# Second self attention of a perceiver block: 64x64 score blocks, and another order of one loop on one Trainium2 core

## The reference

```python
qkv = einsum('bsh,oh->bso', x, w_qkv)      # 32 query heads, 4 key and 4 value heads, each 64 wide
q, k = rope(q, pos), rope(k, pos)          # rotary embedding; k, v are shared by 8 query heads
scores = einsum('bqhd,bkhd->bhqk', q, k) * 64 ** -0.5
scores = where(tril(64, 64), scores, lowest)
out = einsum('bhqk,bkhd->bqhd', softmax(scores), v)
return einsum('bso,ho->bsh', out.reshape(b, s, 2048), w_o)
```

## Time and profile before

| | us |
|---|---|
| median of 3 runs (2544.1 to 2547.37) | 2544.89 |
| the profiled execution's own time | 2557.27 |
| its span | 2555.5 |
| TensorE's matmuls busy in the span | 2288.6 (90%) |
| VectorE busy | 1629.1 (64%) |
| ScalarE busy | 1206.9 (47%) |
| GpSimd busy | 1034.5 (40%) |
| mean granted TensorE clock | 0.941 |

### The profile page before, as it was taken

The page is one execution under the profiler, slowest core; times in us unless marked ns, Lnnn a source line. Parts: engine busy times, 40 slices in busy tenths (PEclk is TensorE's granted clock), DMA queues, the critical chain, the costliest instruction groups (busy, mean ns, idle before and its releaser), DMA issues. The chain is left out here.

```text
span 2555.5 us, 45882 instructions
## 1 busy us (share of the span) xinstructions
PE 2288.6 (90%) x16212; PEld 1813.5 (71%) x16212; DVE 1629.1 (64%) x2618; ACT 1206.9 (47%) x2236; POOL 1034.5 (40%) x718
## 2 busy tenths in 40 slices
PE   4799999999996999969979999999999988888766
PEld 2677777777763888857757788888888866666644
DVE  5367887777785333334422788888788864666663
ACT  2355665666542333313213676666666652233242
POOL 4168988898882000001100455455444530011320
PEclk8799999999996999979999999999999988899889
DMA  3000000001001122114230000000000011111200
GB/s 111 26 2 27 27 27 12 17 27 48 2 1 35 62 66 66 37 22 95 66 108 17 27 27 18 12 27 27 19 10 27 1 66 39 38 37 33 80 1 17
DMA packets 104280, 89.92 MB, mean 35 GB/s; under 512 B 32752, under 2 KB 82432, under 8 KB 104080
## 3 DMA queue, kind: packets, MB, share of 16 engines
q1 hardware_dynamic: 103792, 87.28, 11.3%
q0 software_dynamic: 288, 0.00, 0.0%
HBM read 86.22 MB, written 1.05 MB: 34 GB/s over the span
## 5 line engine op out<-in xcount | busy, mean ns | idle before, releaser
L2276 POOL TENSOR_TENSOR xT<-xT,x1b_ring 128x512 f32<-128x512 f32 (+1 forms) x176 | 248.4, 1411 | 212.6 <-ACT x1b_ring L2406 205.7
L941 POOL TENSOR_TENSOR x0b_krstd<-x0b_krstd,minus_half 128x24 f32<-128x24 f32 x64 | 267.5, 4180 | 88.3 <-DVE x0b_krstd L1004 84.7
L961 POOL TENSOR_TENSOR xT<-xT,x0b_ring 128x512 f32<-128x512 f32 (+1 forms) x170 | 240.3, 1413 | 40.1 <-ACT x0b_ring L1178 25.4
L111 DVE TENSOR_TENSOR x1b_plo<-x1b_ring,x1b_phi 128x512 fp32r<-128x512 f32 (+1 forms) x208 | 222.0, 1067 | 5.3 <-issue 4.7
L2421 ACT ACTIVATE x1b_ring<-x_ps,x1b_keymask 128x512 f32<-128x512 f32 (+1 forms) x208 | 143.1, 688 | 130.5 <-DVE xT L2348 125.8
L1178 ACT ACTIVATE x0b_ring<-x0b_ring 128x512 f32<-128x512 f32 (+1 forms) x208 | 131.2, 631 | 150.1 <-DVE x0b_ring L1022 141.7
L1054 DVE TENSOR_TENSOR x0b_ring<-x_ps,x0b_krstd 128x512 f32<-128x512 f32 (+1 forms) x208 | 142.8, 686 | 75.4 <-PE x_ps L846 74.3
L116 PE MATMUL x_ps<-x1b_qy,x1b_yT 128*128 128x512 f32 (+1 forms) x416 | 175.1, 421 | 4.3 <-ACT x1b_ring L2421 2.9
L2348 DVE SCALAR_TENSOR_TENSOR xT<-x_ps,x1b_keymask,xT 128x512 f32<-128x512 f32 (+1 forms) x176 | 131.2, 746 | 57.6 <-PE x_ps L118 56.7
L116 PE MATMUL x_ps<-x1b_phi,x1b_yv 128*128 128x512 f32 (+1 forms) x416 | 165.8, 399 | 1.5 <-ACT x1b_out_sb L2388 1.5
L118 PE MATMUL x_ps<-x1b_qy,x1b_yT 128*128 128x512 f32 (+1 forms) x416 | 163.9, 394 | 0.0
(11 more groups left out here) (588 smaller groups left out, 5760.5 us busy)
## 6 DMA issues: line engine op xcount, KB each, us to landing
x_y<-in_ctx_dram SPq DMA_DIRECT2D x8, 1536.0 KB
x_y<-in_ctx_dram SPq DMA_DIRECT2D x24, 512.0 KB, 3.9
a_wn<-in_L_attn_W_Q_dram SPq DMA_DIRECT2D x16, 256.0 KB, 3.1
a_wn<-in_L_attn_W_K_dram SPq DMA_DIRECT2D x16, 256.0 KB, 3.4
a_wn<-in_L_attn_W_V_dram SPq DMA_DIRECT2D x16, 256.0 KB, 4.0
a_won<-in_L_attn_W_O_dram SPq DMA_DIRECT2D x16, 256.0 KB, 2.8
x1a_wq<-in_L_xattn_Wq_dram SPq DMA_DIRECT2D x4, 1024.0 KB, 10.6
x1c_wo<-in_L_xattn_Wo_dram SPq DMA_DIRECT2D x8, 512.0 KB, 6.9
```

What stands on the lines that cost most here:

```text
L111: return v.tensor_tensor(lo, exact, hi.bitcast(F32), ALU.subtract)
L941: ins = g_.tensor_tensor(r, r, c.minus_half[:, 0:8].unsqueeze(1).broadcast_to([P, whole, 8]), ALU.pow)
L961: g_.tensor_tensor(total[half][0:m, :], old, src, ALU.add).then_inc(summed, 1)
L2276: g_.tensor_tensor(total[half][0:m, :], old, src, ALU.add).then_inc(summed, 1)
```

## The change

The scores, their softmax and the probabilities keep only the 64x64 blocks within a sequence. S makes for each tile, head and sequence one 64x64 block, the second sequence of a tile on partitions 64 to 127 of the result, so that logits and probabilities are 128 x (4 x 64). The mask is loaded in two pieces of 64x64. F transposes two tiles' probabilities at once, so that keys of even tiles come to lie on partitions 0 to 63 and those of odd tiles on 64 to 127. C makes the values in the same places, in 64 token pieces. V multiplies first the even tiles and then, after a wait for its own first half, the odd ones, since both write the same partitions of the bank. In the order, Q goes ahead of V (and of C), and W ahead of R.

```diff
--- before.py
+++ after.py
@@ -2534,10 +2534,10 @@
         qT = [st.sb(f"qT{i}", [P, B * S]) for i in range(2)]
         kT = st.sb("kT", [P, B * S])
         vn = st.sb("vn", [P, T * HDR])
-        pT = [st.sb(f"pT{u}", [P, T * P]) for u in range(2)]
-        causal = st.sb("causal", [P, P])
+        pT = [st.sb(f"pT{u}", [P, T * S]) for u in range(2)]
+        causal = st.sb("causal", [P, S])
         ln = NormTranspose(st, c, ps)
-        sm = SmallSoftmax(st, HDR ** -0.5, causal[:, :].unsqueeze(1).broadcast_to([P, T, P]))
+        sm = SmallSoftmax(st, HDR ** -0.5, causal[:, :].unsqueeze(1).broadcast_to([P, T, S]), keys=S)
         wn_loaded = [st.sem(f"wn_loaded{u}") for u in range(2)]
         won_loaded = [st.sem(f"won_loaded{u}") for u in range(2)]
         kv_loaded, tables_loaded, zeroed = st.sem("kv_loaded"), st.sem("tables_loaded"), st.sem("zeroed")
@@ -2552,6 +2552,7 @@
         rotated = st.sem("rotated")
         apart = st.sem("apart")
         projected = st.sem("projected")
+        begun = st.sem("begun")
         full = [st.sem(f"full{i}") for i in range(4)]
         free = [st.sem(f"free{i}") for i in range(4)]
 
@@ -2564,9 +2565,10 @@
                     for w in text.split()]
 
 
-        HEAD = "N R1 R0 W O F0 F1 G S V C Q"
-        INNER = "N R0 W O F0 F1 G S V Q"
-        TAIL = "N R0 W A0 O F0 F1 G A1 S"
+
+        HEAD = "N W R1 R0 O F0 F1 G S Q V C"
+        INNER = "N W R0 O F0 F1 G S Q V"
+        TAIL = "N W R0 A0 O F0 F1 G A1 S"
         PAIRS = KVR * PAIRSR
         STEPS = KVR - 1
 
@@ -2574,10 +2576,10 @@
 
 
             if part == "prologue":
-                return (window(1, "A0 A1 W") + window(2, "B") + window(1, "Q") + window(2, "R1 R0 W G S C Q")
-                        + window(3, "N R0 W G F0 F1 S V Q"))
+                return (window(1, "A0 A1 W") + window(2, "B") + window(1, "Q") + window(2, "W R1 R0 G S C Q")
+                        + window(3, "N W R0 F0 F1 G S Q V"))
             if part == "body":
-                return (window(0, INNER) + window(1, TAIL) + window(2, "B") + window(1, "V Q") + window(2, HEAD)
+                return (window(0, INNER) + window(1, TAIL) + window(2, "B") + window(1, "Q V") + window(2, HEAD)
                         + window(3, INNER))
             return (window(0, INNER) + window(1, "N R0 O F0 F1 G S V") + window(2, "N O F0 F1 V")
                     + window(3, "O"))
@@ -2652,9 +2654,12 @@
 
                 load_kv(0)
                 load_query(0, 0)
-                for dst, src in ((turn, c.tables["turn"]), (cosine, c.tables["cosine"]), (sine, c.tables["sine"]),
-                                 (causal, c.tables["causal"])):
+                for dst, src in ((turn, c.tables["turn"]), (cosine, c.tables["cosine"]), (sine, c.tables["sine"])):
                     sp.dma_start(dst[:, :], src).then_inc(tables_loaded, 16)
+
+                for b in range(2):
+                    sp.dma_start(causal[S * b:S * b + S, :], c.tables["causal"][S * b:S * b + S, S * b:S * b + S]
+                                 ).then_inc(tables_loaded, 16)
                 load_query(1, 1)
                 load_out(0, 0)
                 load_out(1, 1)
@@ -2671,7 +2676,7 @@
             @block.gpsimd
             def _(g_):
                 ln.gpsimd(g_)
-                g_.wait_ge(tables_loaded, 64)
+                g_.wait_ge(tables_loaded, 80)
 
                 def body(part, i, first):
                     for off, op, k in plan(part):
@@ -2695,7 +2700,7 @@
                 pe.wait_ge(ln.xT_done, T)
                 pe.wait_ge(x_done, T)
                 pe.wait_ge(zeroed, 1)
-                pe.wait_ge(tables_loaded, 64)
+                pe.wait_ge(tables_loaded, 80)
                 for t in range(T):
                     pe.matmul(ps[:, 4 + t, :], zeros[:, :], xT[0][:, 0, :], start=True, stop=False,
                               skip_group_check=True)
@@ -2742,10 +2747,14 @@
                         if op == "C":
                             pe.wait_ge(kv_done, 2 * g + 2)
                             pe.sem_inc(apart, 1)
-                            for t in range(T):
+
+                            for n in range(T):
                                 for j in range(DC):
-                                    mm = pe.matmul(out[:, t * HDR:(t + 1) * HDR], c.xT[:, j, t * P:(t + 1) * P],
-                                                   wvT[:, j, :], start=(j == 0), stop=(j == DC - 1))
+                                    for r in range(2):
+                                        token = (4 * (n // 2) + 2 * r + n % 2) * S
+                                        mm = pe.matmul(out[r * S:r * S + S, n * HDR:(n + 1) * HDR],
+                                                       c.xT[:, j, token:token + S], wvT[:, j, :],
+                                                       start=(j == 0), stop=(j == DC - 1))
                             mm.then_inc(done, 1)
                         if op == "R":
                             pe.wait_ge(plain_done, rotation_no(part, i, off, k) + 1)
@@ -2757,27 +2766,38 @@
                             for t in range(T):
                                 for half in range(2):
                                     rows = slice(HDR * half, HDR * half + HDR)
-                                    mm = pe.matmul(outs[half][0][:, t * P:(t + 1) * P], qT[u][rows, t * P:(t + 1) * P],
-                                                   kT[rows, t * P:(t + 1) * P], start=True, stop=True)
+                                    for b in range(2):
+                                        at = slice(t * P + b * S, t * P + b * S + S)
+                                        mm = pe.matmul(outs[half][0][b * S:b * S + S, t * S:(t + 1) * S],
+                                                       qT[u][rows, at], kT[rows, at], start=True, stop=True)
                                     if t == T - 1:
                                         mm.then_inc(sm.scores_ready, 1)
                         if op == "F":
                             pe.wait_ge(sm.probs_ready, 2 * m + k + 1)
                             pe.sem_inc(apart, 1)
-                            for t in range(T):
-                                mm = pe.transpose(out[:, t * P:(t + 1) * P], sm.probs[k][:, t, :], c.ident[:, :])
+                            pairs = sm.probs[k][:, :, :].rearrange("p t k -> p (t k)")
+                            for s in range(T // 2):
+                                mm = pe.transpose(out[:, s * P:(s + 1) * P], pairs[:, s * P:(s + 1) * P], c.ident[:, :])
                             mm.then_inc(done, 1)
                         if op == "V":
                             for half in range(2):
                                 wait_copied(pe, part, i, (off, "F", half))
                             pe.wait_ge(v_done, g + 1)
                             pe.sem_inc(apart, 1)
-                            for t in range(T):
-                                for half in range(2):
-                                    mm = pe.matmul(out[HDR * half:HDR * half + HDR, t * P:(t + 1) * P],
-                                                   vn[:, t * HDR:(t + 1) * HDR], pT[half][:, t * P:(t + 1) * P],
-                                                   start=True, stop=True)
-                            mm.then_inc(done, 1)
+                            for r in range(2):
+
+                                if r:
+                                    pe.wait_ge(begun, m + 1)
+                                    pe.sem_inc(apart, 1)
+                                keys = slice(r * S, r * S + S)
+                                for n in range(T):
+                                    s, b = n // 2, n % 2
+                                    at = slice((2 * s + r) * P + b * S, (2 * s + r) * P + b * S + S)
+                                    for half in range(2):
+                                        mm = pe.matmul(out[HDR * half:HDR * half + HDR, at],
+                                                       vn[keys, n * HDR:(n + 1) * HDR],
+                                                       pT[half][keys, n * S:(n + 1) * S], start=True, stop=True)
+                                mm.then_inc(done if r else begun, 1)
                         if op == "O":
                             pe.wait_ge(z_done, m + 1)
                             pe.wait_ge(wo_done, m + 1)
@@ -2829,7 +2849,7 @@
                             act.sem_inc(v_done, 1)
                         if op == "F":
                             act.sem_inc(sm.probs_flipped, 1)
-                            act.activation(pT[k][:, :], src, ACT.Copy).then_inc(done, 1)
+                            act.activation(pT[k][:, :], src[:, 0:T * S], ACT.Copy).then_inc(done, 1)
                         if op == "V":
                             act.activation(zT[u][0][:, :], src, ACT.Copy).then_inc(z_hi, 1)
 
@@ -2846,7 +2866,7 @@
                     v.wait_ge(x_hi, t + 1)
                     rows = slice(t * P, (t + 1) * P)
```

(4 more changed lines are left out.)

## The result

The changed kernel takes 2515.25 us (median of 4, 2508.71 to 2518.95); the kernel before, run beside it, 2546.13 (4, 2544.1 to 2549.37). The ratio is 0.9863, 95% interval 0.9839 to 0.9888: 30.9 us faster, inside the predicted range of 2484 to 2518, and 16 us over the forecast of 2499. The profiled execution took 2508.71 us, against 2557.27 before.

What follows compares the result with a forecast made beforehand. Softmax operations on VectorE and ScalarE that TensorE waits for were taken to set the period. Terms -32.6, -6.4, -5.4, -2.0 and +0.7 sum to -45.7 us, giving 2499 us from the median 2544.89; 8 in 10 range 2484 to 2518.

Steps and rivals of the forecast that it cites:

- the middle: Twelve head pairs, three loop passes, of the second self attention: 194.2 us now, forecast 3 x 10.85 = 32.6 us less.
- ordinary: Head pair without extra projection or weight reading, score product to score product: 11.2 us forecast, against 15.24.
- with B: Pair with the keys' projection and two turnings: 16.3 us forecast against 16.95, little gain, TensorE idle 2.8 us.
- Pairs 0 to 2: Stage's first pairs, 31.27 us now: 6.4 us less, from values' projection at half clock, transposes and one ordinary pair.
- the last interval: Between the last two score products: 16.20 to 10.8 us, 5.4 less, with no more weights loaded and an idle time gone.
- VectorE's list: Forecast VectorE times in an ordinary pair: z low to 6.45, softmax's second half to 8.75, turning to 10.8 us.
- On the median of the runs: Last step: the 45.7 us gain, 2557.27 to 2511.6 in the profiled execution, applied to the median 2544.89, giving 2499.
- part 6: New order, Q ahead of V and W ahead of turnings: R's 2.64 us wait for the copy of Q goes.
- (b): Rival, chance 0.05: column strips in S, V and C do not overlap, 0.107 us an instruction; slower, 2558 us.
- (a): Rival, chance 0.12: clock stays as it is, 14 to 18% of the stage at 1.2 GHz; 2512 to 2522 us.
- (c): Rival, chance 0.08: all packs, S at 0.45 us, no half clock, self-wait 0.2 us; 2484 to 2488 us.
- (d): Rival, chance 0.02: the saved work was never on the chain; time within 5 us of now.

Runs made afterwards that it cites:

- third look: Kernel before, unedited, profiled a third time on chip C: execution 2548.97 us, its twelve middle pairs 184.54 us.
- chip A: Group of runs on one chip beside the kernel before (2550.73 us, 23 runs); the changed kernel again took 2517.04 us, 0.9862.
- VectorE's work put back: Changed kernel plus, per head's softmax, two scratch 128x256 additions ahead of the second exponential and one behind: 2534.98 us, 0.9948 of the kernel before.
- C in one strip: Changed kernel with the values' projection doing all of one 64-column strip, then the other: 2527.0 us, 0.9893 of the kernel before.

## Why the prediction was right, and by how much it was off

**The chain was read rightly.** Against the execution that the sum was made from, it was off by 3 us: 2511.6 forecast, 2508.71 measured. That it came so near is partly luck. By the table, the stage itself gave 43.7 of the 45.7 us; the other 5 us of the 48.6 came from work that the edit does not touch and that the sum had at nothing. That part of the span, all but the stage, is 2262.4, 2261.9 and 2265.7 us in the three profiles of the kernel before, and 2256.3 and 2262.7 in the two of the changed one: this execution was a fast one there. The intervals of the middle, forecast and measured (the two of three that agree): ordinary 11.2 and 12.1, with C 12.4 and 12.4, with the new k and v weights 13.0 and 13.1, with B 16.3 and 16.35; a pass 53.9 and 54.4. Pairs 0 to 2: -6.4 forecast, -8.2 measured; the last interval 10.8 and 10.62; behind the last S -2.0 and -1.3; ahead of the first S +0.7 and +2.25, where the clock is 0.72, against 0.75 in the kernel before (+0.4 in the second profile of the changed kernel, also at 0.75).

The ordinary pair is 0.9 us over its forecast, and the rows above show where. VectorE's list had z low ending at 6.45 and the softmax's second half at 8.75, the turning at 10.8. Measured from S they end at 6.7, 9.4 and 11.8: VectorE stands idle for 0.63 us between z low and the first sum, and for 0.34 ahead of the turning, behind W's low part. The list left 0.15 us for the first and nothing for the second, though the same 0.63 stands at that place in the kernel before:

```profile
2329.76 0.69 DVE L261 TENSOR_REDUCE a_rowsum<-a_probs 128x4 f32<-128x512 f32 x1 [0.63 <-DVE a_zT0lo L111]
```

**Mis-sized: the step from one profile to the median.** "On the median of the runs" took a difference against an execution with 27 us at 1.2 GHz in the middle and set it against a median. Against the third look, an execution near the median, the middle is 184.54 - 163.33 = -21.2 where the term says -32.6, and the last interval 13.17 - 10.62 = -2.6 where it says -5.4. These two terms hold 14.2 of the missing 15 us (30.9 measured, 45.7 forecast); the whole stage is 281.4 - 249.4 = -32.0, as the medians differ. With the second profile of the changed kernel, 247.6 us, it would be -33.8. That this look stands for the typical execution is inferred, from three profiles whose times order like their low-clock stretches (2548.97, 2557.27, 2559.33 us; 10, 27, 31 us). The prediction saw that its execution was 12 us over the median, and took the whole 45.7 us, 12 of them among it, off the median as well.

**Wrong: part 6 as a gain.** The order was counted as what takes away the 2.64 us of R. The whole was summed, never the width alone in the old order; that sum would have shown that six operations of 0.42 us let R's wait shrink to 0.73 with no reordering. What the order adds is z low behind B and Q, which the prediction had in its 16.3 without asking what the old order would give there (14.3 on chip A, two of three). It costs 12 us on the blocks (0.9862 against 0.9812) and 0.3% on the full width. So the total is right with one of its two edits working against it.

**The rivals.** (b), strips that don't overlap: refuted by 0.030 us an instruction in C, where it took 0.107; neighbours that share a strip take 0.056. The rule of the Trainium skill (TensorE: Matmul & The Clock Gate, The mechanism), that loads overlap with matmuls in flight only where the row group differs, disagrees with this trace: the strips of C lie on the same rows, and taking turns between them brings 0.056 down to 0.030. The other page of the Trainium skill, TensorEngine Tiling (Array Packing), Key Properties, by which different tiles load and multiply in parallel, agrees with these 0.030 us. (a), the clock stays: not in the changed kernel (0.99), though the two experiments that slowed it, VectorE's work put back and C in one strip, have it again (0.93 and 0.95). (c), all of it packs: S did, 32 instructions in 0.70 us with the last one's end of 0.22, so 0.48 where I had 0.86 without its end. V packed two at once as forecast, but kept its wait: the halves start 0.84 us apart, of which 16 instructions at 0.031 make 0.49 and the wait for itself 0.35, as I took it. (d), that the saved work was never on the chain, fell with the 30.9 us.

**What stays open.** Why the stretches at the lower clock differ so much between executions of the kernel before. The lower clock starts behind the idle time of R, but in the third look the same idle time of 2.64 us stands in a pair with a granted clock of 1.00 throughout. Nor is the gain split cleanly between VectorE's width and the clock that came back with it.

## What to carry to other kernels

Price each edit alone, in the order of work that is there, before a sum is made: a shorter operation may empty the queue that a reordering was meant to pass, and then only the price of the reordering is left. Before a profile is compared with a median, ask how much of the stage ran at the lower clock and how that execution stands to the others; intervals at full clock are what to subtract. And a total that comes near is to be checked part by part, as unchanged work differs by some us between two executions too. Of a product moved behind others, follow its own consumers in the pair where most work stands ahead of it, here the one of four with a second projection.

## What the runs showed of the hardware

- One kernel, unedited, spent about 27, 31 and 10 us at 1.2 GHz in the same twelve pairs (194.25, 195.92, 184.54 us; mean clock 0.93, 0.92 and 0.97), while the shorter loop repeated its time to 0.1 us in two profiles.
- The score instructions of 64 columns, in turn on four 64x64 tiles, lie 0.015 us apart (32 in 0.70 us with an end of 0.22); those of 128 columns on two tiles of 64 rows lay 0.059 apart (16 in 1.16 with an end of 0.27).
- In C, the same 64 instructions take 2.09 us with their two column strips in turn and 3.77 with one strip after the other.
- A wait of TensorE for its own matmuls, between two halves written to the same bank, cost 0.35 us, beside 0.49 for the 16 instructions ahead of it.
